# Decoder layer on one core: first projections in four half banks, and a new order of cross-attention steps, masks and readouts

## The reference, cut to what matters

```python
# 1 self-attention: 16 heads of 32, ALiBi bias, tanh cap, causal
q, k, v = h @ Wq.T + bq, h @ Wk.T + bk, h @ Wv.T + bv
s = 30 * tanh((q @ k.T + slope * (pos_k - pos_q)) / sqrt(32) / 30)
x = x + softmax(where(causal, s, -inf)) @ v @ Wo.T + bo
# 2 cross-attention, one head over 128 memory rows, with a mask
a = softmax(where(mask, (norm(x) @ mem.T) / sqrt(512), -1e30))
x = x + where(any(mask), a @ mem, 0)
# 3 feed-forward, weights rounded to fp8 (e4m3), scales in f32
x = x + (silu(n @ q8(gate) * gs) * (n @ q8(up) * us)) @ q8(down) * ds
```

## Time and profile before

| what | value |
| --- | --- |
| median of 3 executions | 558.46 us |
| profiled execution, device time | 558.21 us |
| its span, first to last instruction | 556.4 us |
| mean granted TensorE clock, share of full speed | 0.996 |
| busy: PEld / DVE / ACT / POOL | 427.4 / 361.7 / 268.5 / 287.1 us |
| chain that ended last, by engine | PE 83%, POOL 8%, DVE 4%, issue 2%, ACT 2%, DMA 1% |

### The profile page before, as it was taken

One profiled execution on the slowest core, in us unless ns is written; L12 is line 12 of the kernel. 1 busy time (PEld: TensorE's weight loads), 2 busy tenths in 40 slices (PEclk: granted clock), 3 DMA queues, 4 the chain that ended last, 5 costly groups with the idle time before them and its releaser, 6 DMA issues.

```text
span 556.4 us, 10168 instructions
## 1 busy us (share of the span) xinstructions
PE 543.5 (98%) x3962; PEld 427.4 (77%) x3962; DVE 361.7 (65%) x699; ACT 268.5 (48%) x485; POOL 287.1 (52%) x260
## 2 busy tenths in 40 slices
PE   7999999999999999999899999999999999999997
PEld 7788888888878888888687888766686667866675
DVE  7998877899596796659777886355623564244422
ACT  6848976777765785765743441033401333023310
POOL 5298898965774568787774346134400333013320
PEclk9999999999999999999899999999999999999999
DMA  8951231463217110148832712100011000100001
GB/s 306 347 199 39 78 99 54 124 194 103 77 39 223 43 58 21 58 153 258 275 150 77 264 26 89 57 1 0 1 38 39 0 1 0 58 19 1 0 20 57
DMA packets 43422, 50.74 MB, mean 91 GB/s; under 512 B 2544, under 2 KB 25072, under 8 KB 43376
## 3 DMA queue, kind: packets, MB, share of 16 engines
q1 hardware_dynamic: 43088, 49.58, 26.8%
q10 hardware_dynamic: 288, 0.52, 0.3%
HBM read 36.46 MB, written 13.63 MB: 90 GB/s over the span
## 4 chain that ended last, share of the span: by engine, by line
PE 83%; POOL 8%; DVE 4%; issue 2%; ACT 2%; DMA 1%; DVEq 0%; ACTq 0%; POOLq 0%
PE bank L287 34%; PE bank L452 23%; PE bank L472 16%; PE bank L282 2%; PE bank L394 2%; PE bank L379 2%; PE bank L404 2%; POOL q_w L740 2%; POOL q_w L738 2%; POOL probs L731 1%; POOL x_res L754 1%; PE bank L334 1%; DVE q_m L1228 1%; PE bank L371 1%; POOL reduced L723 1%
## 5 line engine op out<-in xcount | busy, mean ns | idle before, releaser
L287 PE MATMUL bank<-reduced 128*128 128x512 f32 x936 | 224.4, 396 | 1.5 <-ACT probs L897 1.1
L287 PEld LDWEIGHTS bank<-reduced 128*128 128x128 f32 x936 | 173.8, 189 | 39.8 <-issue 1.5
L837 POOL TENSOR_TENSOR f_parts<-fused,f_parts 128x512 fp32r<-128x512 f32 x48 | 62.5, 1301 | 159.9 <-ACT f_parts L1075 159.9
L1057 ACT ACTIVATE tanh_g<-bank,half_gate 128x512 f32<-128x512 f32 x48 | 33.0, 688 | 149.2 <-PE bank L452 139.0
L472 PE MATMUL bank<-reduced,f_parts 128*128 128x512 f32 x384 | 88.4, 390 | 0.0
L472 PEld LDWEIGHTS bank<-reduced,f_parts 128*128 128x128 f32 x384 | 71.9, 188 | 15.0
L1395 DVE SCALAR_TENSOR_TENSOR silu<-tanh_g,bank 128x512 f32<-128x512 f32 x48 | 32.9, 685 | 62.7 <-ACT tanh_g L1057 62.6
L452 PE MATMUL bank<-reduced 128*128 128x512 f32 x288 | 72.0, 402 | 0.0
L452 PEld LDWEIGHTS bank<-reduced 128*128 128x128 f32 x288 | 54.1, 188 | 12.9
L738 POOL TENSOR_TENSOR q_w<-q_w,q_m 128x512 f32<-128x512 f32 x36 | 49.6, 1379 | 9.2 <-DVE q_m L1230 9.2
L731 POOL TENSOR_SCALAR_AFFINE_SELECT probs<-probs 128x1024 f32<-128x1024 f32 x32 | 36.2, 1136 | 34.6 <-ACT probs L904 34.6
(11 more groups left out here) (119 smaller groups left out, 737.1 us busy)
## 6 DMA issues: line engine op xcount, KB each, us to landing
quantized<-q_w SPq DMA_DIRECT2D x36, 256.0 KB, 3.3
reduced<-quantized SPq DMA_DIRECT2D x12, 512.0 KB, 6.8
memT_sb<-in_memT SPq DMA_DIRECT2D x16, 256.0 KB, 5.1
mem_sb<-in_mem SPq DMA_DIRECT2D x16, 256.0 KB, 5.8
out<-y_sb SPq DMA_DIRECT2D x16, 256.0 KB, 2.0
q_w<-in_gate_w SPq DMA_DIRECT2D x12, 256.0 KB, 3.2
q_w<-in_up_w SPq DMA_DIRECT2D x12, 256.0 KB, 3.1
x_res<-in_x SPq DMA_DIRECT2D x3, 1024.0 KB, 9.4
```

Of the source, the lines that this page charges most:

```text
L287: ins = pe.matmul(dst, stationary, moving, start=(n == 0), stop=(n == len(pairs) - 1))
L837: pool.tensor_tensor(f_lo[:, f, :], fused[:, f % 2, :], f_hi[:, f, :].bitcast(F32), ALU.subtract).then_inc(f_lo_ready, 1)
```

## The change

The change does these things:

- x tiles 0 to 3 are all loaded by SyncE's queue, ahead of the small constants and the weights; ScalarE issues no load.
- The high part of the first 128 columns of Wq is written by GpSimd, after the third reciprocal root, with a semaphore of its own (`w_first_made`); ScalarE keeps that of Wk.
- `first_qk` puts the second halves (tiles 2 and 3) into banks 6 and 7 as items Q2 and K2. ScalarE evicts four halves, the first two as soon as they are filled. `scores(0, 0)` waits for Q2 and K2 only at token tile 2.
- `bias_through` comes after the third V projection in place of the first.
- `gate_up` takes the bank of `up` after it has issued the products of `gate`.
- For g >= 2, VectorE does `cross(g-2, 6)` ahead of the last slabs of head group 0, and `masks(g-1)` moves behind `norm_shift` of head group 1.
- `norm_apply` of tile 0 moves behind the four `x_low`, to the other three tiles. For 0 < g < 3 two tiles' statistics and `cross(g-1, 1)` go ahead of the first slab of head group 3.
- GpSimd does the first half of `causal(g, 2)`, then `low_part(g, 0)`, then the second half, then `norm_scale`.
- At the start of the feed-forward, `cross(2, 1)` moves ahead: on ScalarE before the slab checks and `high(0, 1)`, on VectorE before `fuse(0, 1)` and `normalize_context(3, 3)`. In step 1 ScalarE copies T2 before it does the exponential.

```diff
             def first_qk():
-                banks = [take((name, 0, 0), (Q_BANK, K_BANK)[m]) for m, name in enumerate("QK")]
+                first = [take((name, 0, 0), b) for name, b in (("Q", Q_BANK), ("K", K_BANK))]
+                second = [take((name, 0, 0), b) for name, b in (("Q2", C_BANK), ("K2", E_BANK))]
...
                 pe.wait_ge(xT_hi_ready, 2)
-                for m in range(2):
-                    pe.wait_ge(w_hi_made, m + 1)
-                    part(m, first, w_hi, xT_hi, start=True)
-                    if m == 0:
-                        turn_x(0, 3, S_BANK + 3)
+                pe.wait_ge(w_first_made, 1)
+                part(first, 0, w_hi, xT_hi, start=True)
+                turn_x(0, 3, S_BANK + 3)
+                pe.wait_ge(w_hi_made, 1)
+                part(first, 1, w_hi, xT_hi, start=True)
...
             def scores(g, hg):
                 for i in range(GT):
+                    if g == 0 and hg == 0 and i == 2:
+                        wait_drained(pe, ("Q2", g, hg))
+                        wait_drained(pe, ("K2", g, hg))
...
                     v_proj(g, i, (C_BANK, E_BANK, Q_BANK, K_BANK)[i])
-                    if g == 0 and i == 0:
+                    if g == 0 and i == 2:
                         bias_through()
...  SyncE and ScalarE, loads
-            for i in range(0, GT, 2):
+            for i in range(GT):
                 sp.dma_start(x_res[:, i, :], x_t[:, i, :]).then_inc(x_first_loaded[i], 16)
-            for i in range(1, GT, 2):
-                act.dma_start(x_res[:, i, :], x_t[:, i, :]).then_inc(x_first_loaded[i], 16)
...  GpSimd
+                if i == 2:
+                    pool.wait_ge(raw_loaded[0], 16)
+                    pool.tensor_copy(w_hi[:, 0, :, FIRST], raw[0].rearrange("p (k n) -> p k n", k=KT)[:, :, FIRST])\
+                        .then_inc(w_first_made, 1)
...
+                slabs = slabs_at(ROUNDED, g, 2)
+                causal(g, 2, (0,))
                 if g:
                     low_part(g, 0)
+                causal(g, 2, (2,))
                 if g:
                     norm_scale(1, g - 1)
-                slabs = slabs_at(ROUNDED, g, 2)
-                if g:
                     round_slabs(slabs[:1])
-                causal(g, 2)
...  ScalarE
-            weight_high(0)
             weight_high(1)
...
-            q_out(0, 0)
-            k_out(0, 0)
+            for items in (("Q", "K"), ("Q2", "K2")):
+                for name, dst, bias in zip(items, (qT, kT), (bq_c, bk_c)):
+                    src, cols = wait_filled(act, (name, 0, 0)), slice(0, 2 * S) if name in "QK" else slice(2 * S, TG)
+                    act.activation(dst[:, cols], src[:, cols], ACT.Identity, bias=bias[:, 0:1])\
+                        .then_inc(drain_sem((name, 0, 0)), 1)
...
             gate(0, 1)
+            cross(G - 2, 1)
             flag_slabs(slabs_at(FLAGGED, G - 1, 3))
             high(0, 1)
-            cross_first(G - 2, 1)
...  VectorE
                     cross(g - 2, 5)
+                    cross(g - 2, 6)
                     prepare_slabs(slabs[2:])
-                    cross(g - 2, 6)
-                    masks(g - 1)
...
                     norm_shift(g + 1)
+                    if g >= 2:
+                        masks(g - 1)
...
-                if g:
-                    norm_apply(1, g - 1, g - 1, range(1))
                 prepare_slabs(slabs_at(PREPARED, g, 2))
...
                 if g:
-                    norm_apply(1, g - 1, g - 1, range(1, GT))
+                    norm_apply(1, g - 1, g - 1)
...
             fuse(0, 0)
+            cross(G - 2, 1)
             fuse(0, 1)
             normalize_context(G - 1, 3)
-            cross(G - 2, 1)
```

More of the change, by code:

```diff
@@ L327, in first_qk, with part @@
             def first_qk():
-                banks = [take((name, 0, 0), (Q_BANK, K_BANK)[m]) for m, name in enumerate("QK")]
-                def part(m, cols, w, t, start=False, stop=False):
-                    dst, done = banks[m]
+                first = [take((name, 0, 0), b) for name, b in (("Q", Q_BANK), ("K", K_BANK))]
+                second = [take((name, 0, 0), b) for name, b in (("Q2", C_BANK), ("K2", E_BANK))]
+                def part(half, m, w, t, start=False, stop=False):
+                    (dst, done), cols = half[m], slice(0, 2 * S) if half is first else slice(2 * S, TG)
                     for k in range(KT):
@@ L335, in part @@
                                         stop=stop and k == KT - 1)
-                    return ins, done
-                first, second = slice(0, 2 * S), slice(2 * S, TG)
+                    if stop:
+                        ins.then_inc(done, 1)
                 pe.wait_ge(xT_hi_ready, 2)
-                for m in range(2):
-                    pe.wait_ge(w_hi_made, m + 1)
-                    part(m, first, w_hi, xT_hi, start=True)
-                    if m == 0:
-                        turn_x(0, 3, S_BANK + 3)
+                pe.wait_ge(w_first_made, 1)
[3 more added lines that the diff above has]
+                part(first, 1, w_hi, xT_hi, start=True)
                 for i in range(2):
@@ L347, in first_qk @@
                 for m in range(2):
-                    part(m, first, w_hi, xT_lo)
+                    part(first, m, w_hi, xT_lo)
                 for m in range(2):
                     pe.wait_ge(w_lo_made, m + 1)
-                    part(m, first, w_lo, xT_hi, stop=True)
+                    part(first, m, w_lo, xT_hi, stop=True)
                 pe.wait_ge(xT_hi_ready, GT)
                 for m in range(2):
-                    part(m, second, w_hi, xT_hi, start=True)
+                    part(second, m, w_hi, xT_hi, start=True)
                 for m in range(2):
-                    part(m, second, w_lo, xT_hi)
+                    part(second, m, w_lo, xT_hi)
                 for i in range(2, GT):
@@ L359, in first_qk @@
                 for m in range(2):
-                    ins, done = part(m, second, w_hi, xT_lo, stop=True)
-                    ins.then_inc(done, 1)
+                    part(second, m, w_hi, xT_lo, stop=True)
             def scores(g, hg):
@@ L439, in gate_up @@
                     pe.wait_ge(w16_made, f + 1)
-                seats = [take((name, g, f), banks[w]) for w, name in ((0, "G"), (1, "U"))]
                 if g == 0:
-                    for w, (dst, done) in enumerate(seats):
+                    for w, name in ((0, "G"), (1, "U")):
+                        dst, done = take((name, g, f), banks[w])
                         products(dst[:], [(gu_w[:, PLACES[f], w, k], part[:, k]) for k in range(KT)
@@ L445, in gate_up @@
                     return
+                seats = []
                 for n, high in enumerate((f % 2 == 0, f % 2 == 1)):
-                    for w, (dst, done) in enumerate(seats):
+                    for w, name in ((0, "G"), (1, "U")):
+                        if n == 0:
+                            seats.append(take((name, g, f), banks[w]))
+                        dst, done = seats[w]
                         for k in range(KT):
@@ L724, in low_part, with causal @@
                     .then_inc(ctx_lo, 1)
-            def causal(g, hg):
-                for j in range(0, 4, 2):
+            def causal(g, hg, pairs=(0, 2)):
+                for j in pairs:
                     pool.wait_ge(exped, (g * HG + hg) * 2 + j // 2 + 1)
@@ L949, in cross_second @@
             def cross_second(g, k):
+                if k == 1:
+                    x2_out(g, k)
                 if 0 <= k - 1 < GT:
@@ L1092, in _ @@
                 gate(0, f)
-                if f != 8:
+                if f != 2 and f != 8:
                     cross_second(*step[f - 1])
@@ L1233, in weight_low @@
                 m, cols = W_PARTS[n]
-                dve.wait_ge(w_hi_made, n + 1)
+                if n:
+                    dve.wait_ge(w_hi_made, n)
+                else:
+                    dve.wait_ge(w_first_made, 1)
                 hi, lo = (w_hi[:, m], w_lo[:, m]) if m < 3 else (wo_hi, wo_lo)
@@ L1368, in _ @@
                 if g:
-                    norm_apply(1, g - 1, g - 1, range(1, GT))
+                    norm_apply(1, g - 1, g - 1)
                 normalize_context(g, 2)
                 slabs = slabs_at(PREPARED, g, 3)
[L1373 to L1378, removed]
+                if 0 < g < G - 1:
+                    next_stats(g + 2, range(2))
+                    cross(g - 1, 1)
+                    prepare_slabs(slabs[:1])
+                    next_stats(g + 2, range(2, GT))
+                else:
+                    prepare_slabs(slabs[:1])
+                    if g == 0:
+                        next_stats(g + 2)
                 if g:
```

13 lines of the change are left out of this document (7 added, 6 removed).

## The result

The changed kernel took 551.67 us (median of 6 executions, 551.31 to 551.92) where the kernel before took 557.75: a ratio of 0.988, interval 0.9864 to 0.9896. The forecast was 551.5. The profiled execution took 551.92, its span 549.9 (before 558.21 and 556.4).

A forecast was written before the change was run, and what follows sets the result against it. TensorE, busy 98%, was taken as the bound, so only its waits and low-clock time could be won back: 3.7 + 1.1 + 0.7 + 1.2 = 6.7 us off 558.21 gives 551.5; eight-in-ten range 549.8 to 554.6.

The forecast's parts named there:

- The start of the feed-forward: Moving cross(2, 1) ahead there removes TensorE's 2.27 us wait and the low clock: gain 3.7 us, bounds 2.5 and 4.2.
- the bank took the place: At gate_up(0, 3), a bank 6 wait of 0.5 us remains; as a rival, 1.4 us or more, chance 0.17.
- The wait and the low clock behind it cost 4.22 us: Feed-forward start: the disturbed stretch takes 12.14 us, an undisturbed one with the same work 7.92.
- Group 2: Third head group's Q projection waited for bank 0, drained by cross(0, 6)'s readout; moving that ahead gains 1.1 us.
- the releaser's name was false: In group 2 the profile names a tanh for the 1.13 us wait; the prediction blamed bank 0's late drain.
- Group 1: Third head group: context(1, 2) waited for the causal halves; reordering GpSimd gains 0.7 us (0.5 to 0.7).
- TensorE would ask at 114.2: Group 1: when TensorE wants context(1, 2), with the second causal half expected done at 113.4.
- The opening: Four edits gain 1.55 us in front, about 1.2 at context(0, 1); rival that the gain is lost, chance 0.15.
- the front moves with it: Opening: x tile 0 lands 0.4 us earlier, and all that follows VectorE's statistics moves earlier too.
- the 0.4 for the loads: Opening: loading all x tiles on one queue brings tile 0 0.4 us earlier, bounds 0 and 1.1.
- The 0.3 for the copy: Opening: Wq's high part on GpSimd instead of ScalarE gains 0.3 us, bounds -0.9 to 0.57.
- the 0.85 for the half evictions: Opening: evicting first projections in halves cuts 2.15 us before the next Q product to 1.3, gaining 0.85.

The follow-up runs named there:

- one_queue_alone: The kernel before with only the x loads changed, all four tiles on SyncE's queue: 0.25 us less, no gain the interval tells.
- cross_late: The changed kernel with cross(2, 1) back in its old place on ScalarE and VectorE: 554.28 us against 551.67 and 551.38.
- cross_alone: The kernel before with only cross(2, 1) moved ahead on ScalarE and VectorE, and step 1's T2 copy ahead of the exponential: 0.52% (2.9 us) gained.
- readout_late: The changed kernel with cross(g-2, 6) on VectorE behind head group 0's last slabs again: 552.63 us against 551.38.
- three_moves: The changed kernel with bias_through behind the first V projection, low_part ahead of both causal halves, the second gate's tanh ahead of high(0, 0): 550.38 us.
- after_again: The changed kernel itself measured once more, as the yardstick for later runs: 551.38 us.
- copy_on_act: The changed kernel with the high part of Wq's first columns back on ScalarE: 551.55 us against 551.67.
- busy_wait: The kernel before with nine dummy-product calls put in TensorE's 2.27 us feed-forward wait, no wait removed: 0.19% (1.1 us) gained.
- two_queues: The changed kernel with x tiles 1 and 3 loaded by ScalarE's queue again: 1.3 us over the changed kernel's median.

## Why the prediction was right, and where its sizes were off

**The start of the feed-forward: right.** Forecast 3.7, measured 3.76 between the two traces (12.14 to 8.38); the bank took the place, with 0.31 us and not 0.5. The added steps cost little because VectorE had room: it stood 1.27 us for the tanh of the second gate before, and 0.76 after. What the working left out is that the low clock is not certain. "The wait and the low clock behind it cost 4.22 us" came again in the trace of one_queue_alone (12.12 us for the stretch) and, by the mean clock, in most executions of the kernel before; but cross_late had a longer wait and no low clock. In medians the move is worth 2.9 us in the kernel before (cross_alone, whose trace lost some in the opening and behind the stretch) and 2.6 to 2.9 in the changed one (cross_late).

**Group 2: right**, 1.13 us in the trace and 1.25 by readout_late, and so was the reading that the releaser's name was false.

**Group 1: half.** 0.38 of 0.7 us. "TensorE would ask at 114.2" overlooked a second condition: context(1, 2) needs bank 6 too. Its drain waits in `normalize_context(1, 1)` for `low_part(1, 0)`, which the change put behind the first causal half (until 112.07), so the shuffles began at 112.19 and not in time. With `low_part` first, in three_moves, no wait is left there.

**The opening: the sum too large, for the wrong path.** Of the 1.2 us that were to come out at `context(0, 1)`, 0.91 did, and 0.60 was left at `context(0, 3)`; in the trace of after_again it is 1.31 and 1.01. The step that failed is "the front moves with it". Tile 0 landed 0.6 us sooner, but tile 2 later: VectorE stood 0.64 us for it, until 6.32, where it had read it at 6.19 without a wait. The path to the first product goes through tile 2 normed (turned at 8.96) and the six dummy products behind it, which the working did not have. So the 0.4 for the loads hangs on when tile 2 lands: it came out as 0.03 here, 0.39 in after_again (VectorE stood 0.34 us for that tile) and 0.53 in one_queue_alone (it did not stand), by the start of the first product. The 0.3 for the copy was 0 (copy_on_act), and the 0.85 for the half evictions was 0.86. Of `bias_through` VectorE's wait was foreseen, and it was 0.91 us: with the front only 0.86 earlier its product came late, and the output bias ran at 32.51, not at 31.8. I had put the cost at `context(0, 1)`. A wait of 0.34 us showed at `context(0, 2)`, which three_moves took away; that `bias_through` made it is likely, and was not tested by itself.

**What was not in the prediction** is the clock of the opening. The gain is 6.1 us by the medians of the result, 7.1 beside after_again and 6.5 between the traces, and these differ because single executions do. The four places give 3.76 + 1.13 + 0.38 + 0.60 = 5.87 of the 6.5 us of span. The other 0.6 came in small steps that the working did not have, such as a wait of 0.20 us for VectorE's addition to x before the row at 305.62, which is gone. That they make up for most of what the opening and group 1 fell short is luck. The changed kernel is the steadier one, 0.8 us from lowest to highest of its 10 executions, against 3.2 us in the first six of before. Two places where the clock varies are seen in traces with the old order or the old queues: behind the 2.27 us wait and in the opening. That one queue makes the opening steady is shown for the changed kernel only. Why the same edit alone did not tell in the median of the kernel before stays open; its slowest of 12 executions took 558.30, where the kernel before beside it reached 560.82.

**What no run tested alone**: `gate_up`'s later take, the move of the masks and that of `norm_apply`.

The rule of the Trainium skill ("SBUF — State Buffer", Who interferes with whom) on the exclusive port pair did not decide anything: GpSimd's copy took 0.61 us beside VectorE's steps, near the 0.55 of the forecast.

## What to carry to other kernels

When TensorE is 98% busy, list each of its waits and, for each, every semaphore and bank that the waiting instruction needs; the profile names only one of them, and the name can be wrong: for the same wait it was the tanh in two traces and the readout in three. The next one in the list is what the edit will meet. Compare two stretches with the same work to price a wait, since a lowered clock behind it is in no wait's figure, and look at several executions before that price is called the kernel's. In an opening, look for the dummy work and the last tile on the path before moving loads or conversions.

## What the runs showed of the hardware that I had not expected

- A TensorE wait of 2.27 us was followed by 1.2 GHz in two traces (granted clock 0.50 from 272.5 to 275.5 in before, and from 271.5 in one_queue_alone), one of 2.65 us in cross_late was not. By the mean clock, 11 of 13 executions of the kernel before had it, and one of four of cross_late.
- Dummy products inside the wait kept the clock up (busy_wait): 8.31 us for the work behind it in place of 9.87.
- In an opening with the x tiles on two queues (two_queues) the granted clock stood at 0.50 from 9 to 11 us, and the executions fell in two lots 1.5 us apart.
- The granted clock of a trace does not show every slow opening: in cross_alone its windows from 8 to 11 us say 1.00, yet four transposes took 0.81 us, as in two_queues at 0.50 and not as in before (0.53).
- Four transfers of 256 KB on one queue landed less evenly than on two. The first came after 2.8 us and not 3.4, but VectorE's wait for the third was anything from 0 (one_queue_alone, three_moves) to 0.87 us (cross_late), where on two queues it had none.
